# A decoder layer on one core: one folded product moved in one piece behind a later tile of x, and a weight split moved with it

## The reference

```python
x = layernorm(x + attn(x))          # linear attention: no softmax
x = layernorm(x + xattn(x, ctx))    # 16 heads, softmax over 154 context rows, mask
x = layernorm(x + ffn(x))           # r * (relu(k)**2 @ Wv), token-shifted inputs

# attn, without softmax:
attn = einsum('bhik,bhjk->bhij', q, k)
out = einsum('bhik,bhkj->bhij', attn, v)   # = q (k' v), so per batch it folds into a matrix
return out @ w_o.T + b_o
```

## Time and profile before

| | us |
|---|---|
| median of 3 runs | 919.35 (919.19 to 919.79) |
| the profiled execution | 921.59 |
| its span in the trace | 919.8 |
| PE busy | 901.9 (98%) |
| DVE busy | 727.7 (79%) |
| ACT busy | 557.5 (61%) |
| POOL busy | 506.9 (55%) |

### The profile page before, as it was taken

One profiled execution on the slowest core, in us unless ns is written; L12 is line 12 of the kernel. 1 busy time (PEld: TensorE's weight loads), 2 busy tenths in 40 slices (PEclk: granted clock), 3 DMA queues, 4 the chain that ended last, 5 costly groups with the idle time before them and its releaser, 6 DMA issues.

```text
span 919.8 us, 19153 instructions
## 1 busy us (share of the span) xinstructions
PE 901.9 (98%) x6758; PEld 743.7 (81%) x6758; DVE 727.7 (79%) x2007; ACT 557.5 (61%) x1676; POOL 506.9 (55%) x505
## 2 busy tenths in 40 slices
PE   9979999999999999999999999999999999999997
PEld 7868787778888878787878888878787878787876
DVE  6689686677887879797978888787878787879775
ACT  7563526868675656565757575666665757575631
POOL 1035015758684747576665757566665666656420
PEclk9989999999999999999999999999999999999999
DMA  8672020114000000002000010101010100100001
GB/s 289 232 242 72 23 74 23 42 43 126 9 24 31 25 31 24 31 24 87 25 31 25 24 31 24 31 25 31 24 31 24 29 26 10 45 2 24 2 24 46
DMA packets 31033, 45.65 MB, mean 50 GB/s; under 512 B 2779, under 2 KB 15579, under 8 KB 30811
## 3 DMA queue, kind: packets, MB, share of 16 engines
q1 hardware_dynamic: 27339, 37.36, 12.6%
q10 hardware_dynamic: 3600, 7.08, 2.3%
HBM read 34.10 MB, written 9.70 MB: 48 GB/s over the span
## 4 chain that ended last, share of the span: by engine, by line
PE 74%; DVE 5%; issue 3%; POOL 3%; ACT 1%; POOLq 0%; ACTq 0%
PE dense L88 18%; PE dense L90 17%; PE dense L89 17%; PE turned L1628 5%; PE scores L1616 4%; PE rest_value L1642 4%; PE rest_value L1646 3%; PE dense L1515 2%; PE turned L1515 1%; PE rest_value L1634 1%; POOL row_inv L1421 1%; POOL prob L1427 1%; DVE stats L1108 1%; DVE prob L1149 1%; DVE gate_then_y L1216 0%
## 5 line engine op out<-in xcount | busy, mean ns | idle before, releaser
L1421 POOL TENSOR_TENSOR row_inv<-row_sum,minus_one 128x4 f32<-128x4 f32 x128 | 145.7, 1138 | 254.7 <-ACT prob L830 253.3
L830 ACT ACTIVATE prob<-prob,row_min 128x154 f32<-128x154 f32 x512 | 209.4, 417 | 17.8 <-DVE row_min L1149 17.8
L1427 POOL TENSOR_TENSOR prob<-prob,row_inv 128x512 f32<-128x512 f32 x128 | 141.9, 1109 | 0.0
L1149 DVE CUSTOM_DVE_ANT_0 prob<-scores,mask_add 128x154 f32<-128x154 f32 x512 | 127.0, 309 | 0.7 <-PE scores L1616 0.7
L838 ACT ACTIVATE prob_t<-turned 128x512 f32<-128x512 f32 x128 | 76.0, 593 | 56.9 <-PE turned L1628 56.8
L830 ACT ACTIVATION_READ_ACCUMULATOR prob<-prob,row_min 128x1 f32 x512 | 99.0, 193 | 0.0
L1628 PE MATMUL turned<-ident,prob 128*128 128x128 f32 x512 | 77.0, 273 | 1.3 <-ACT prob_t L838 0.8
L88 PE MATMUL dense<-xt_hi,cross_wq_hi 128*128 128x256 f32 x256 | 74.7, 292 | 0.5 <-DVE xt_lo L1140 0.5
L88 PE MATMUL dense<-mix_k_hi,ffn_wk_hi 128*128 128x256 f32 x256 | 74.5, 291 | 0.0
L1207 DVE TENSOR_TENSOR k_act_lo<-square,k_act_hi 128x512 fp32r<-128x512 f32 x32 | 50.3, 1571 | 28.3 <-ACT k_act_hi L863 28.3
L89 PE MATMUL dense<-xt_lo,cross_wq_hi 128*128 128x256 f32 x256 | 72.3, 282 | 0.0
(11 more groups left out here) (305 smaller groups left out, 2751.1 us busy)
## 6 DMA issues: line engine op xcount, KB each, us to landing
x_rows<-x_rows SPq DMA_DIRECT2D x32, 256.0 KB, 3.7
xt_raw<-x_cols SPq DMA_DIRECT2D x16, 512.0 KB, 3.7
out<-gate_then_y SPq DMA_DIRECT2D x15, 512.0 KB, 2.8
mask_in<-mask SPq DMA_DIRECT2D x16, 154.0 KB, 2.4
cross_wv<-cross_wv SPq DMA_DIRECT2D x2, 512.0 KB, 6.8
cross_wk<-cross_wk SPq DMA_DIRECT2D x1, 1024.0 KB, 9.5
self_wk<-self_wk ACTq DMA_DIRECT2D x1, 1024.0 KB, 7.8
cross_wq_raw<-cross_wq ACTq DMA_DIRECT2D x1, 1024.0 KB, 10.8
```

The costliest lines, as they stand in the source:

```text
L830: m = act.activation(keys, keys, ACT.Exp, bias=row_min[:, buf, t, h:h + 1], scale=-1.0, accum_out=row_sum[:, buf, t, h:h + 1])
L1149: m = dve.tensor_tensor_reduce(prob[buf][:, t, h * CTX:(h + 1) * CTX], s_bank[:, h, t * CTX:(t + 1) * CTX], mask_add[n % 2][:, t, :], -SCA ...
L1421: pool.tensor_tensor(row_inv[:, buf, t, :], row_sum[:, buf, t, :], minus_one[:], ALU.pow).then_inc(*p_inv.up)
L1427: pool.tensor_tensor(keys[:, :, 0:P], keys[:, :, 0:P], inv.broadcast_to([P, HPG, P]), ALU.mult).then_inc(*p_norm.up)
```

## The change

It moves work within the prologue's programs. No instruction is added or taken away.

- PE: the four parts of T run in one piece behind tile 25. Tile 26 follows, then K'V, then tiles 27 and 28, U, and tiles 29 to 31. Before, T stood in two pieces behind tiles 21 and 23, and K'V behind tile 25.
- PE: the 12 matmuls of T's part 0 come in another order, such that those with the weights' low part are the last four, and only they wait for it. The wait ahead of T is for the weights' high part.
- ACT: the high part of `self_wv` is made behind `sums_high(0)`, ahead of tile 22, and no longer between tiles 15 and 16. The high parts of `cross_wq`, `cross_wo` and `self_wq` each move by two tiles.
- DVE: the low part of `self_wv` comes behind tile 25. The order behind it is: tile 26, `s_part`, tile 27, T parts 0 and 1, `cross_wq`, tiles 28 and 29, `cross_wo`, T parts 2 and 3, `self_wq`, tile 30, K'V's copies, tile 31.

```diff
@@ ACT
-            high(14, 15)
-            weight_high("self_wv")
-            high(16, 17)
+            high(14, 15, 16, 17)
             take_sums(0)
...
             sums_high(0)
+            weight_high("self_wv")
             high(22, 23)
             load_row("self_bo")
+            high(24, 25)
             for i, name in enumerate((*early, "self_wq")):
                 weight_high(name)
-                high(2 * i + 24, 2 * i + 25)
-            high(30, 31)
+                high(2 * i + 26, 2 * i + 27)
@@ DVE
-            low(*range(10, 16))
-            weight_low("self_wv")
-            low(16, 17)
+            low(*range(10, 18))
...
             sums_low(0, *range(KT))
+            low(22, 23)
             take_columns(0)
+            low(24, 25)
+            weight_low("self_wv")
+            low(26)
...
-            low(22, 23)
+            low(27)
             take_t(0, 1)
             weight_low("cross_wq")
-            low(24, 25)
+            low(28, 29)
             weight_low("cross_wo")
             take_t(2, 3)
-            low(26, 27)
             weight_low("self_wq")
-            low(28)
+            low(30)
...
-            low(29, 30, 31)
+            low(31)
@@ PE, t_product
+                    if i == 0:
+                        for g_part, w_part in ((0, 0), (1, 0), (0, 1)):
+                            if w_part:
+                                pe.wait_ge(*w_low.at(place_of("self_wv")))
+                            for k in range(KT):
+                                m = pe.matmul(t_bank[i][:], g_two[0][g_part][:, k, 0:P], self_wv_two[w_part][:, k, :],
+                                              start=(g_part + w_part + k == 0), stop=(w_part == 1 and k == KT - 1))
+                    else:
...
@@ PE
-            sums(20, 21)
-            pe.wait_ge(*w_low.at(place_of("self_wv")))
+            sums(20, 21, 22, 23, 24, 25)
+            pe.wait_ge(*w_high.at(place_of("self_wv")))
             pe.wait_ge(*g_whole.at(0))
-            t_product(0, 1)
-            sums(22, 23)
             pe.wait_ge(*s_ok.at(0))
-            t_product(2, 3)
-            sums(24, 25)
+            t_product(0, 1, 2, 3)
+            sums(26)
...
-            sums(26, 27, 28)
+            sums(27, 28)
```

More of the change, by code:

```diff
@@ L514, in t_product @@
                 for i in parts:
-                    for k in range(KT):
-                        m = three_pass(pe, t_bank[i][:], [x[:, k, i * P:(i + 1) * P] for x in g_two[0]],
-                                       [x[:, k, :] for x in self_wv_two], first=(k == 0), last=(k == KT - 1))
+                    if i == 0:
[6 more added lines that the diff above has]
+                    else:
+                        for k in range(KT):
+                            m = three_pass(pe, t_bank[i][:], [x[:, k, i * P:(i + 1) * P] for x in g_two[0]],
+                                           [x[:, k, :] for x in self_wv_two], first=(k == 0), last=(k == KT - 1))
                     m.then_inc(*t_mm.up)
```

## The result

The changed kernel takes 924.95 us (923.06 to 926.16, 4 runs), the kernel before 919.47 (919.19 to 919.79, 4 runs): ratio 1.0058, 95% interval 1.004 to 1.0076. That is +5.5 us, against +3.8 forecast; the interval, in us, is +3.7 to +7.0. 924.95 lies in the stated range of 917.5 to 926.0, 1.9 us over the likeliest value, 923.1. In a second series it was 925.82 against 919.85, ratio 1.0056 (1.0042 to 1.0071).

The account below looks back on a forecast made before the run. PE, busy for 98% of the span, was taken to bound the kernel. K'V 3.6 us later less 1.5 for a tile gave +2.1; with +1.7 for the clock, 919.35 + 3.8 = 923.1 us, range 917.5 to 926.0.

Parts of the forecast that it names:

- The bound moves from PE to DVE's list, with the last take_t at its end: Prologue: DVE's work up to the last take_t holds K'V until 86.6 us, leaving PE idle for 5 to 7 us.
- the sign of being wrong: Start of K'V in the changed profile: before 84.5 us would speak against the forecast.
- The early part's gain: PE up to tile 21: holes of 0.56 and 1.89 us ahead of tiles 16 and 21 go; 0.7 us taken up to tile 20.
- DVE's own work, 21.4 us: DVE from the end of take_mirror's additions to the last take_t: 21.4 us of its own instructions, without POOL's delays.
- POOL's additions, ten of 1.1 us: Additions of tiles 22 to 31 during DVE's list: each delays DVE by 1.1 us, 11.2 us in all.
- a lock from shared bandwidth: DVE and POOL in SBUF: one engine fully blocks the other for an instruction; shared bandwidth would make the price less.
- Late tiles on top: DVE's list: no late-tile wait in the sum; only the additions' upper bound, 12.5 us, included a late tile.
- rival 3: self_wq's early load holds tiles 22 to 24 back; K'V at 88.6 us, at half clock, total 926; chance 0.12.
- The clock at K'V, 1.7 us: PE's idle time ahead of K'V lowers its clock, costing 1.7 us, bounds 0 to 4.4.
- The work between the two earlier holes: PE in the kernel before, between holes of 1.89 and 2.50 us: 1.7 us of work.
- The sum: Whole kernel: +2.1 us from K'V's later start less one tile, +1.7 for the clock, together +3.8.
- the likeliest case's own range: Total time if the main forecast holds: 921.8 to 925.0 us, around 923.1; chance 0.50.

Follow-up runs that it names:

- e2: Changed kernel with DVE's take_t 2 and 3 put ahead of the cross_wq, cross_wo and self_wq splits, no work left out: 917.40 us, ratio 0.9961.
- e6: Kernel before with only the split of self_wv moved, T left in two pieces: 919.56 us, ratio 0.9994.
- e1: Changed kernel with POOL's additions of tiles 20 to 31 cut to one column: 916.48 us, ratio 0.9949 to the kernel before.
- e3: Changed kernel with 17 unused matmuls of 512 columns on PE behind tile 26, filling the hole ahead of K'V: 923.86 us.
- e9: Kernel before with 7 unused matmuls behind tile 20 and 10 behind tile 21, filling its two holes: 919.84 us against 919.99.
- e4: Changed kernel with self_wv split between tiles 15 and 16, as in the kernel before: 925.56 us.
- e5: Changed kernel run again unedited, beside other kernels on another chip: 925.82 us.

## Why the prediction was right, point by point

- **The bound moves from PE to DVE's list, with the last take_t at its end.** Right. The hole ahead of K'V is 4.29 and 6.74 us (5 to 7 forecast), released by take_t; e2 takes most of it away by order alone. K'V starts at 84.53 and 86.00, forecast 86.6; the first is only just on the right side of the 84.5 that I had named as the sign of being wrong.
- **The early part's gain.** Right in its places: no hole ahead of 16 and 21, 2.00 us ahead of tile 22 (2.0 forecast). e6 doesn't show it worth anything by itself in the median.
- **DVE's own work, 21.4 us.** Measured without POOL's additions: 21.6 (e1).
- **POOL's additions, ten of 1.1 us.** The size was somewhat high (and ten times 1.1 is 11.0, not 11.2). In the first profile the list is 31.3 us, of which 31.3 - 21.6 - 1.3 = 8.4 are additions; in the second 53.71 to 85.9 = 32.2, less 21.6 and 1.5 of waiting, 9.1. Added up from the rows of the first profile, each less what the same work takes in e1, it is 8.5. So eight or so count. Tiles 24 and 25's cost 0.67 and 0.54 us in the first profile (rows of 1.35 and 1.22 us for a low part of 0.68), since they began while DVE waited for ACT. One that cost nothing is tile 31's: it started at 78.94, stood through the splits and the low parts of tiles 28 and 29, and ran beside take_t, for 5.35 us in all (POOL's timeline):

```profile
63.88 9.63 POOL L466 TENSOR_TENSOR x_sum<-x_sum,x_rows 128x512 f32<-128x512 f32 x5 [0.25 <-DMA x_rows<-x_rows]
78.94 5.35 POOL L466 TENSOR_TENSOR x_sum<-x_sum,x_rows 128x512 f32<-128x512 f32 x1 [5.42 <-DMA x_rows<-x_rows]
```

In the second profile tiles 28 and 29 took 2.35 us at 80.08, with that addition between them, and K'V came later for it. "Each addition delays DVE by 1.1 us, however it falls" was therefore too strong: which of the two engines goes next varies from run to run. Nor does a price of 1.1 us alone tell a lock from shared bandwidth, as the prediction had it. The long rows tell more: an addition that waits 4 us at no cost to DVE, here and in e1, where one of a single column took 4.31 us and ended at 78.30, just behind the start of take_t at 78.17.
- **Late tiles on top.** I gave rival 3 the loads; they are a small term of the list, 1.3 to 1.5 us of waiting for tiles 24 and 25, that I had put at nothing. It makes up for part of the additions that were too many.
- **The clock at K'V, 1.7 us.** 5.92 - 4.38 = 1.54 in the first profile; in the second K'V takes 86.00 to 92.75 = 6.75 us, 2.37 more than 4.38. e3 shows that the hole causes it. Within the bounds, the term up to 0.7 too small. The work between the two earlier holes, called 1.7 us, is 2.15 in the trace (59.51 to 61.66); nothing in the sum hangs on it.
- **The sum.** +3.8, against +1.5 and +3.8 between the profiled executions and +5.5 between the medians. DVE's list ends at 84.4 and 85.9 us against the 86.5 of the sum: it starts 0.8 and 0.2 us earlier, its own work is 0.2 more, the additions are 2.8 and 2.1 less, and 1.3 and 1.5 of waiting come on top. The last step failed: I carried a difference between profiled executions over to the medians. The profiled execution of the kernel before, 921.59, is 2.1 over its median of 919.47, that of the changed one 1.9 under its own. They lie on opposite sides within their kernels' runs (918.6 to 923.9 over all series for the kernel before, 923.1 to 926.3 for the changed one), so the base of my sum was off by some 2 us. Even so 924.95 lies in the stated range; that it lies in the likeliest case's own range, 921.8 to 925.0, by 0.05 us, is luck; the second series' 925.82 is outside it, and inside the wider one. I had thought that the low clock behind T's hole sets the profiled execution apart. e9 and the runs' clocks say that it is a part of the kernel before's spread and not all of it. How much is due to it, and how much to POOL's additions falling among DVE's instructions by chance, remains open; the row of 5.78 us in e9 is one case of the second.

## What to carry to other kernels

Before work is packed together on the bound engine, add up what the helper engine must do ahead of its last hand-over, each instruction with what contends with it; here the list was 4 to 7 us longer than PE's. If it is longer, put the hand-over first and the splits that nobody waits for behind it: the same work took 7.5 us less here. And a single profiled execution is one draw from the kernel's runs: where a sum is made against it, its distance from the median belongs in the range.

## What the runs showed of the hardware that was not expected

- An addition of POOL that reads SBUF can wait through several of DVE's instructions and not only one: 5.35 us, from 78.94 to 84.3, against 1.27 for one undisturbed. DVE lost nothing to it. In e1 one of a single column took 4.31 us, against 0.19. Both ended once DVE had come to take_t, which reads PSUM. In the changed kernel's next profile the same addition got in between two low parts and cost DVE 1.1 us.
- With the hole ahead of K'V filled up to its last 1.50 us, K'V is at full clock (eight matmuls in 1.16 us); with the hole open at 4.29 us they take 2.08. Behind holes of 1.40 (e2) and 1.88 us (e4) K'V is at full clock too. Ahead of tile 22 the length doesn't decide: holes of 2.00 (the changed kernel's first profile) and 2.01 us (e3) go with a mean clock of 0.83 from 58 to 68 us, holes of 1.99 (e5) and 2.01 us (e2) with 1.00.
